# Building the adjacency: four of five tiles' slot one-hots scaled on ScalarE instead of three

## The chip, the cores and the metric

The kernel is one program on one core of a Trainium2 chip. The metric is the device time of one execution in microseconds (us). In the profile the engines are PE (TensorE matmuls), PEld (TensorE weight loads), DVE (VectorE), ACT (ScalarE), POOL (GpSimd) and SP (SyncE, which issues most DMAs).

## The reference

A two-stage graph network on 12500 nodes with 64 features and 412500 edges (`src`, `dst`, sorted by `dst`), cut to what matters:

```python
h = relu(layernorm(x))
x = x + hypergraph_conv2(h, (src, dst), W1, b1, W2, b2)   # segment sums over src and dst
h = relu(layernorm(x))
# e  = silu(silu([h[src], h[dst], edge_weight1] @ eW1 + eb1) @ eW2 + eb2)
# agg = segment_sum(e, src);  x = x + silu([h, agg] @ nW1 + nb1) @ nW2 + nb2
```

The change touches only the first stage of the kernel, called building here: it sorts the edges of each chunk of nodes into buckets, and counts them into blocks of the adjacency matrix, which the later stages read.

## The kernel before

Building takes the first 3.3 ms. It runs over 49 chunks (a turn of the loop each). A chunk holds `TC = 70` tiles of 128 edges, taken as `NGR = 14` groups of `GT = 5` tiles. Each engine has its own instruction stream, written by hand, and waits for the others on semaphores; nothing reorders the streams. I call the work that an engine's loop body does for one value of g a slot, so a turn has slots 0 to 13. For group g:

- **POOL** (`onehots`, L621) writes `OH`, for each edge a one-hot over 102 bucket keys.
- **PE** (`ranks`, L731 to L739) sums these into `R`, the running rank of each edge in its bucket. It does so one slot ahead.
- **ACT** copies the carry out of it (`count`, `cb`, L859) and widens `OH` to fp32 (`widen`, `OHf`, L865).
- **DVE** (`ranks`, L968 and L970) reduces `R` to the rank `rk` of each edge. Then `places` writes the slot one-hots of the group. For the first `AT` tiles it writes an unscaled bf16 one-hot `LB` (L981). For the others it writes `LH` itself, in one instruction a tile (L987): two one-hots, scaled by the edge's two payloads `pl`.
- **ACT** (`scaled`, L875) makes `LH` of the first `AT` tiles out of `LB`, with two activations a tile, one for each payload.
- **PE** (`buckets`, L753) multiplies `OHf` by `LH` into the sorted chunk `S`, with ten matmul rows a group, one slot later: in slot g + 1 it does `buckets` of group g.

The width of a one-hot, `WIDE[t]`, grows from 16 in the first tile to 128 in the last ones.

Between these, each of slots 2 to 13 has three or four units of the previous chunk (slots 0 and 1 have four each, the last of a chunk). For a unit, DVE writes the one-hots `OB`, `OA`, `OD` (L1038 to L1046, two units at a time), PE counts them into a PSUM bank (`counts`, L778, L779), ACT copies the bank into `RB` (`keep`, L911), and PE uses `RB` of a unit three back in `sums` (L794). At the end of a chunk DVE (`filled`, L999) and ACT (`record`, L882) empty `S`.

The order inside a slot matters below. PE in slot g: `ranks(g + 1)`, units 1 and 2, `buckets(g - 1)`, the other one or two units. ACT in slot g: `count(g + 1)`, `widen(g)`, `keep` of all units of the slot, then `scaled(g)`. DVE in slot g: two units, `ranks(g)`, one unit, `places(g)`, the rest. `LB`, `LH`, `OHf` and `cb` have two buffers each.

```python
for k in range(AT):                       # scaled, ACT, L871
    for c in range(2):
        ins = e.activation(LH[g % 2][:, k, c, 0:w], LB[g % 2][:, k, 0:w], ACT.Copy, scale=pl[:, c, t:t + 1])
ins.then_inc(a_lh, 1)
e.wait_ge(v_lh, i * NGR + (g + 1))        # buckets, PE, L745
e.wait_ge(a_of, i * NGR + (g + 1))
e.wait_ge(a_lh, i * NGR + (g + 1))
```

Of the kernel before, what the change touches and what calls it, by code (L numbers as in the profile page):

```python
# [20 lines left out]
TC = 70  # L21
CAP = TC * P
GT = 5
AT = 3
TWO = 2.0 ** -9
NGR = TC // GT
KEYS = 102
# [38 lines left out]
def gnn_kernel(nc, x, src, dst, ew, W1, b1, W2, b2, eW1, eb1, eW2, eb2, nW1, nb1, nW2, nb2, out):  # L66
# [14 lines left out]
    with root:  # L81
# [34 lines left out]
        def past(e, s, v):  # L116

            if not isinstance(v, int) or v > 0:
                e.wait_ge(s, v)

        def sbt(ctx, name, shape, dt):
            return ctx.enter_context(nc.sbuf_tensor(name, shape, dt))
# [353 lines left out]
        with tz:  # L476
            p1 = ExitStack()
            with p1:
# [7 lines left out]
                LH = [sbt(p1, f"LH{n}", [P, GT, 2, P], fp32) for n in range(2)]  # L486
                LB = [sbt(p1, f"LB{n}", [P, AT, P], bf16) for n in range(2)]
                OHf = [sbt(p1, f"OHf{n}", [P, GT, KEYS], fp32) for n in range(2)]
# [82 lines left out]
                with nc.Block() as block:  # L571
# [283 lines left out]
                    def _(e):  # L855
# [11 lines left out]
                        def scaled(i, g, pl):  # L867

                            e.wait_ge(v_lb, i * NGR + (g + 1))
                            past(e, p_s, i * NGR + (g - 1))  # L870
                            for k in range(AT):  # L871
                                t = g * GT + k
# [80 lines left out]
                    def _(e):  # L953
# [19 lines left out]
                        def places(i, g, pl):  # L973
# [4 lines left out]
                            past(e, a_lh, i * NGR + (g - 1))  # L978
                            for k in range(AT):
                                t = g * GT + k  # L980
                                ins = e.tensor_scalar(LB[g % 2][:, k, 0:WIDE[t]], iot1[:, 0:WIDE[t]], float(OWN - 1), rk[:, t:t + 1], ALU.add, ALU.is_equal)  # L981
                            ins.then_inc(v_lb, 1)
                            for k in range(AT, GT):
                                t = g * GT + k
# [1540 lines left out]
```

## Time and profile before

| | us |
|---|---|
| median of 3 runs | 9332.65 |
| lowest and highest | 9325.49, 9347.12 |
| the profiled execution, its own time | 9347.07 |
| its span | 9345.3 |

The span is the time from the first to the last instruction of the profiled execution. It lies 1.8 us inside that execution's own time, and that execution lies 14.4 us over the median. "Busy" counts the time in which an engine has an instruction at work; the ends of matmuls are modelled, their starts are recorded. Rows of the trace of before stand further down, in numbered groups.

### The profile page before, as it was taken

Reading aid. Unit: us, or ns where it says so; the run is one execution under the profiler, and the core shown is the slowest. Engines: PE = TensorE matmul, PEld = TensorE weight load, DVE = VectorE, ACT = ScalarE, POOL = GpSimd, SP = SyncE. Lnnn points to the kernel's source line nnn. Section 1 sums busy time; section 2 is a strip of 40 time slices with the busy share of each in tenths; the row PEclk is TensorE's granted clock in tenths of the full one; section 3 lists DMA queues with packets and bytes.
Section 4 is the critical chain, followed back from the end, with each engine's and each line's share of the span. In section 5 each row is a group of like instructions: output and inputs, shape, how many; then the busy total and the mean of one; then the engine's idle time right before and its main releaser. Section 6 shows DMA issues by size and latency. Waiting matters only on the chain. (4 is left out here: it accounts for less than half of the span.)

```text
span 9345.3 us, 289343 instructions
## 1 busy us (share of the span) xinstructions
PE 8577.7 (92%) x95106; PEld 7679.0 (82%) x95890; DVE 7760.4 (83%) x21596; ACT 5344.2 (57%) x14224; POOL 2985.7 (32%) x4177
## 2 busy tenths in 40 slices
PE   3999999999999989998888999599999999999997
PEld 2777777777777769998888998489989899999895
DVE  8999999999999976775888886478888888888884
ACT  3777777777777750001777786245555555555552
POOL 5877777777777830000000000011111111111110
PEclk9999999999999999997999998599999999999998
DMA  2666666666666677664999997533333333333332
GB/s 74 149 150 149 152 148 152 148 151 148 151 148 151 149 172 193 190 190 114 228 222 211 240 241 168 129 98 92 97 93 92 97 91 97 93 94 97 89 97 72
DMA packets 1475613, 1312.43 MB, mean 140 GB/s; under 512 B 829932, under 2 KB 1211094, under 8 KB 1473636
## 3 DMA queue, kind: packets, MB, share of 16 engines
q1 hardware_dynamic: 1444438, 1270.13, 56.3%
q0 software_dynamic: 28224, 26.62, 1.1%
q8 instruction: 739, 12.11, 0.5%
q14 instruction: 372, 3.05, 0.1%
q10 hardware_dynamic: 1840, 0.53, 0.0%
HBM read 777.40 MB, written 361.77 MB: 122 GB/s over the span
## 5 line engine op out<-in xcount | busy, mean ns | idle before, releaser
L621 POOL TENSOR_SCALAR OH<-iot,kd 128x102 bf16<-128x102 bf16 x3440 | 2334.1, 698 | 61.7 <-PE S L753 61.4
L2170 POOL DMA_INDIRECT Qx<-tab_q,tidx x294 | 407.5, 1386 | 5231.9 <-DVE skt L2204 2602.0
L1425 PE MATMUL wp<-AF,XS 128*128 128x256 f32 x9604 | 1214.6, 285 | 157.5 <-issue 121.7
L1425 PEld LDWEIGHTS wp<-AF,XS 128*128 128x128 f32 x9604 | 1165.9, 191 | 189.0 <-issue 188.8
L911 ACT ACTIVATE RB<-PS 128x256 int16<-128x256 f32 x2401 | 898.6, 381 | 639.9 <-PE PS L779 591.6
L1451 ACT ACTIVATE AF<-RG 128x1536 fp32r<-128x1536 uint8 x686 | 1022.6, 1491 | 340.9 <-PE wp L1425 208.0
L794 PE MATMUL HP<-T3a,RB 128*128 128x193 bf16 x9604 | 1187.3, 246 | 27.3 <-ACT RB L911 27.3
L753 PE MATMUL S<-LH,OHf 128*102 128x256 f32 (+14 forms) x6860 | 1160.5, 316 | 50.3 <-ACT LH L875 29.6
L2191 ACT ACTIVATE Z<-Zb 128x512 f32<-128x512 f32 x882 | 556.2, 631 | 991.6 <-DVE Zb L2249 987.6
L875 ACT ACTIVATE LH<-LB,pl 128x128 f32<-128x128 bf16 (+14 forms) x4116 | 1113.1, 356 | 0.0
L753 PEld LDWEIGHTS S<-LH,OHf 128*102 128x102 f32 x6860 | 921.7, 169 | 195.9 <-issue 96.1
L2249 DVE TENSOR_TENSOR Zb<-p,eb2s 128x512 f32<-128x512 f32 x882 | 609.9, 692 | 535.5 <-PE p L2143 502.1
L2143 PE MATMUL p<-eW2s,Y 128*128 128x128 f32 x7056 | 928.3, 274 | 48.9
L794 PEld LDWEIGHTS HP<-T3a,RB 128*128 128x128 fp8e4 x9604 | 851.7, 97 | 128.7 <-issue 39.8
L1505 DVE CAST AF<-RG 128x2048 fp32r<-128x2048 uint8 x686 | 813.3, 1222 | 155.7 <-DMA RG<-adjT 64.6
L2143 PEld LDWEIGHTS p<-eW2s,Y 128*128 128x128 f32 x7056 | 922.9, 191 | 24.1
L1046 DVE TENSOR_TENSOR OD<-iot,SBd 128x512 bf16<-128x512 bf16 x2401 | 937.4, 428 | 0.0
L2125 PEld LDWEIGHTS pT<-OdT,ACC 128*128 128x128 bf16 x21756 | 792.6, 97 | 162.1 <-issue 162.1
L2184 ACT ACTIVATE Y<-pT,eb1s 128x512 f32<-128x512 f32 x882 | 606.0, 687 | 494.8 <-PE pT L2125 462.8
L2125 PE MATMUL pT<-OdT,ACC 128*128 128x84 bf16 (+10 forms) x21756 | 853.0, 196 | 0.0
L1290 PE MATMUL hp<-ACC,RG 128*128 128x193 bf16 x9604 | 822.3, 247 | 4.0 <-DMA RG<-adjT 4.0
L1290 PEld LDWEIGHTS hp<-ACC,RG 128*128 128x128 fp8e4 x9604 | 815.0, 98 | 8.1 <-issue 4.5
(329 smaller groups left out, 16065.5 us busy)
## 6 DMA issues: line engine op xcount, KB each, us to landing
RG<-adjT SPq DMA_DIRECT2D x1372, 224.0 KB, 7.0
adj<-RB SPq DMA_DIRECT2D x343, 448.0 KB, 2.8
adjT<-RT SPq DMA_DIRECT2D x686, 224.0 KB, 3.7
RG<-adj SPq DMA_DIRECT2D x686, 224.0 KB, 4.6
sdb<-bk SPq DMA_DIRECT2D x196, 768.0 KB
sdb<-bk SPq DMA_DIRECT2D x98, 384.0 KB
sdb<-bk SPq DMA_DIRECT2D x98, 261.0 KB
WR<-wk SPq DMA_DIRECT2D x882, 9.0 KB
```

The costliest lines, as they stand in the source:

```text
L621: ins = e.tensor_scalar(OH[:, g * GT + k, :], iot1[:, 0:KEYS], kd[:, g * GT + k:g * GT + k + 1], None, ALU.is_equal)
L753: ins = e.matmul(slots_to(w), lhsT=OHf[g % 2][:, k, :], rhs=LH[g % 2][:, k, :, 0:w], start=False, stop=True, skip_group_check=True)
L794: ins = e.matmul(HP[:, h * W3:(h + 1) * W3], lhsT=pair[:, x_, h * P:(h + 1) * P], rhs=T3a[:, 2 * (u - 1) + x_, :], start=False, stop=True, ...
L875: ins = e.activation(LH[g % 2][:, k, c, 0:w], LB[g % 2][:, k, 0:w], ACT.Copy, scale=pl[:, c, t:t + 1])
L911: e.activation(RB[n % NSLOT][:, k, :].bitcast(i16), bank(u)[:, 0:256], ACT.Copy, accum_out=gs[:, u:u + 1]).then_inc(a_u, 1)
L1046: ins = e.tensor_tensor(OD[k % PAIRS][:, y, :, :], iot2[:, :, :], SBd[:, b + 2 * y:b + 2 * y + 2].unsqueeze(1).to_broadcast([P, 256, 2]), ...
L1290: ins = e.matmul(ps[b][:, h * W:(h + 1) * W], lhsT=piece(n, k_, h), rhs=tin3[:, n * 2 * PIECE + k_, 0:W], start=False, stop=True, skip_gro ...
L1425: ins = e.matmul(ps[b][:, 0:256], lhsT=XS[:, n * PB + m, :, :].rearrange("p c f -> p (c f)"), rhs=AF[:, (b + n) % 3, m, :], start=n == 0 a ...
L1451: e.activation(floats((b + n) % 3, VB, PB), counts(n, VB, PB), ACT.Copy).then_inc(h_ca, 1)
L1505: e.tensor_copy(floats((b + n) % 3, 0, VB), counts(n, 0, VB)).then_inc(h_cd, 1)
L2125: ins = e.matmul(o[:, a:b], lhsT=v[:, n, c, :], rhs=D_[:, h, a:b], start=False, stop=True, skip_group_check=True)
L2143: ins = e.matmul(p2[g % 2][:, t * P:(t + 1) * P], lhsT=Y[g % 2][:, t * P:(t + 1) * P], rhs=nW["eW2s"][:, :], start=True, stop=True)
```

## The change

`AT` goes from 3 to 4. `LB` grows by one tile, to `[P, AT, P]`.

```diff
@@ -21,7 +21,7 @@
 TC = 70
 CAP = TC * P
 GT = 5
-AT = 3
+AT = 4
 TWO = 2.0 ** -9
 NGR = TC // GT
 KEYS = 102
```

In each group the fourth tile's scaled pair, which one DVE instruction wrote (with `iofo`, an index row offset by 255), is now one bf16 one-hot from DVE and two activations on ACT. PE, POOL and SP keep every instruction in its place.

ACT, slots 12 and 13 of a turn in the loop (`RB` is `keep` of a unit, `LH<-LB,pl` is `scaled`), the second of them with four units:

```order
 L911 ACTIVATE RB,rows_of<-PS 128x256 x3
-L875 ACTIVATE LH<-LB,pl 128x128 x6
-L859 ACTIVATE cb<-R 128x102
-L865 ACTIVATE OHf<-OH 128x510
-L911 ACTIVATE RB,rows_of<-PS 128x256 x4
-L875 ACTIVATE LH<-LB,pl 128x128 x6
+L875 ACTIVATE LH<-LB,pl 128x128 x8
+L859 ACTIVATE cb<-R 128x102
+L865 ACTIVATE OHf<-OH 128x510
+L911 ACTIVATE RB,rows_of<-PS 128x256 x4
+L875 ACTIVATE LH<-LB,pl 128x128 x8
```

Each run of six activations is now a run of eight, and the signal that it is done comes with the eighth; the copy of the carry (`cb`) for the next group stands behind it.

DVE, slot 12 of the same loop (`LB` is the unscaled one-hot, `LH` the scaled pair, `OB` begins the next two units):

```order
-L981 TENSOR_SCALAR LB<-iot,rk 128x128 x3
-L987 SCALAR_TENSOR_TENSOR LH<-iofo,rk,pl 128x256
+L981 TENSOR_SCALAR LB<-iot,rk 128x128 x4
 L987 SCALAR_TENSOR_TENSOR LH<-iot,rk,pl 128x256
 L1038 TENSOR_SCALAR OB<-iot,SBk 128x128 x2
```

One instruction has taken the place of another; the signal for `LB` comes one instruction later, that for `LH` behind as many instructions as before.

## Rows read from the trace of the kernel before

**Rows 1.** The page: busy us, share of the span and instructions of each engine.

```profile
PE 8577.7 (92%) x95106; PEld 7679.0 (82%) x95890; DVE 7760.4 (83%) x21596; ACT 5344.2 (57%) x14224; POOL 2985.7 (32%) x4177
```

**Rows 2.** Busy time by stretch: bounds, length, engines, granted PE clock, DMA share, GB/s.

```profile
2000.00:2500.00 500.00, 474.96 (x4070) 393.03 (x4068) 480.30 (x2055) 389.60 (x1627) 380.21 (x566) 1.00 0.68 151
```

**Rows 3.** Timeline of PE, slots 12 and 13: start, length, instruction, idle before it.

```profile
1989.67 2.38 PE L753 MATMUL S<-LH,OHf 128*102 128x256 f32 x10 [0.36 <-ACT LH L875]
...
2051.56 2.32 PE L753 MATMUL S<-LH,OHf 128*102 128x240 f32 x10
...
2055.74 0.50 PE L794 MATMUL HP<-T3a,RB 128*128 128x193 bf16 x4
2056.60 2.38 PE L753 MATMUL S<-LH,OHf 128*102 128x256 f32 x10 [0.36 <-ACT LH L875]
```

**Rows 4.** Timeline of ACT in the same slots.

```profile
2049.59 1.82 ACT L875 ACTIVATE LH<-LB,pl 128x120 f32<-128x120 bf16 x6
...
2054.24 0.38 ACT L911 ACTIVATE RB<-PS 128x256 int16<-128x256 f32 x1 [1.44 <-PE PS L779]
...
2054.61 1.85 ACT L875 ACTIVATE LH<-LB,pl 128x128 f32<-128x128 bf16 x6
2056.36 0.23 ACT L859 ACTIVATE cb<-R 128x102 bf16<-128x102 f32 x1
```

**Rows 5.** Waits in building, 1000 to 3000 us (30 turns): total us, times, longest.

```profile
ACT RB L911 <- PE PS L779: 361.8, 390, 1.5
...
PEld S L753 <- issue: 56.7, 184, 0.6
...
PE PS L778 <- DVE OD L1046: 49.3, 60, 1.1
...
DVE rk L968 <- ACT cb L859: 32.1, 30, 1.1
...
PE S L753 <- ACT LH L875: 17.5, 60, 0.4
```

**Rows 6.** Groups of building by line (0 to 3300 us): count, busy us, mean ns.

```profile
L875 ACT ACTIVATE LH<-LB,pl 128x16 f32<-128x16 bf16 (+3 forms) x3990 | 1078.0, 356 | 0.0
...
L981 DVE TENSOR_SCALAR LB<-iot,rk 128x128 bf16<-128x128 bf16 (+14 forms) x1998 | 408.0, 267 | 25.1 <-DVE rk L970 17.5 <-PE S L753 3.9
...
L987 DVE SCALAR_TENSOR_TENSOR LH<-iofo,rk,pl 128x256 f32<-128x256 f32 (+11 forms) x666 | 257.8, 387 | 0.0
```

**Rows 7.** Timeline of DVE in slot 12: `places`, and the pair behind it.

```profile
2051.01 0.58 DVE L981 TENSOR_SCALAR LB<-iot,rk 128x128 bf16<-128x128 bf16 x3
2051.50 0.47 DVE L987 SCALAR_TENSOR_TENSOR LH<-iofo,rk,pl 128x256 f32<-128x256 f32 x1
2051.90 0.48 DVE L987 SCALAR_TENSOR_TENSOR LH<-iot,rk,pl 128x256 f32<-128x256 bf16 x1
```

**Rows 8.** Timeline of ACT: `scaled` of groups 2, 7 and 0, and what follows.

```profile
2007.81 1.42 ACT L875 ACTIVATE LH<-LB,pl 128x40 f32<-128x40 bf16 x6
2009.13 0.24 ACT L859 ACTIVATE cb<-R 128x102 bf16<-128x102 f32 x1
...
2029.38 1.65 ACT L875 ACTIVATE LH<-LB,pl 128x88 f32<-128x88 bf16 x6
...
2066.49 1.32 ACT L875 ACTIVATE LH<-LB,pl 128x16 f32<-128x16 bf16 x6
2067.69 0.27 ACT L859 ACTIVATE cb<-R 128x102 bf16<-128x102 f32 x1
```

**Rows 9.** Timeline of PE: where it waits for DVE, and `buckets` of groups 2 and 7.

```profile
2009.38 1.11 PE L753 MATMUL S<-LH,OHf 128*102 128x80 f32 x10 [0.23 <-ACT LH L875]
...
2019.81 0.29 PE L778 MATMUL PS<-OD,OA 128*128 128x256 bf16 x1 [0.93 <-DVE OD L1046]
...
2030.90 0.29 PE L778 MATMUL PS<-OD,OA 128*128 128x256 bf16 x1 [0.79 <-DVE OD L1046]
...
2032.03 1.71 PE L753 MATMUL S<-LH,OHf 128*102 128x176 f32 x10
```

## The prediction

> **What bounds the kernel now.** I read the busy shares first. Over the whole span PE is busiest, then DVE [rows 1], but the change lies in building alone, so the shares of that stretch count: of 500 us there, DVE is busy 480 and PE 475, while ACT is busy 390, or 78% [rows 2]. Read so far, DVE looks like the bound and ACT like the engine with room. A share does not say which wait ends last, so I went to the order of time.
>
> The turns repeat: `buckets` of group 12 starts at 1989.67 and again at 2056.60, 66.93 us apart [rows 3]. What releases it can be read from two timelines. ACT's six scaling activations of group 11 end at 2049.59 + 1.82 = 2051.41, and `buckets(11)` starts at 2051.56. Those of group 12 end at 2054.61 + 1.85 = 2056.46, and `buckets(12)` starts at 2056.60. Both times PE starts 0.14 to 0.15 us behind ACT's last activation [rows 3, 4]. It could have started sooner: four `sums` matmuls that began at 2055.74 take about 0.34 us from start to start, so PE was free at about 2056.1, and the profile gives the 0.36 us in between to `LH` of ACT [rows 3]. And ACT did not dawdle: it waited 1.44 us for PE's counts of the slot's last unit, copied them, and began to scale at once [rows 4].
>
> So in the late slots PE and ACT form a closed loop: `buckets` of one group, counts of the slot's last units, ACT's `keep`, ACT's `scaled`, `buckets` of the next group. DVE is not in it: its one-hots of group 12 stood from 2052.4 on, over 2 us before ACT read them [rows 7, 4]. The summed waits support this and also warn: PE's wait for `LH` is only 17.5 us in 30 turns, but another 56.7 us in 184 pieces, six a turn, stands at the same line under "issue" [rows 5], a name for idle time with no visible releaser. I take those for the same wait. ACT idles 361.8 us in 30 turns, all of it waiting for PE's counts [rows 5]. That is ACT's 22% of room, and it lies ahead of `keep`. The added work lies behind `keep`, so it cannot go there.
>
> DVE does set the time at two places of a turn: PE waits 0.93 us for `OD` at 2019.81 and 0.79 us at 2030.90 [rows 9], 49.3 / 30 = 1.64 us a turn on average [rows 5].
>
> **The change part by part.** *ACT, two activations more a group.* From the start of `scaled` to the start of the next instruction six activations take 1.32 us in slot 2 (2007.81 to 2009.13) and 1.75 us in slot 12 (2054.61 to 2056.36) [rows 8, 4]. The twelve distances of slots 2 to 13 grow with the width between these and sum to 18.85 us. Two more of eight cost a third of that: 6.28 us in twelve slots, of which slots 8 to 13 have 3.39. The group row gives the same size: 1078.0 / 3990 = 0.27 us each [rows 6], times 24 is 6.5.
>
> *DVE, one instruction exchanged a group.* `LB` costs 408.0 / 1998 = 0.20 us, the pair 0.387 us [rows 6]: 0.18 us saved a group, 2.6 us a turn. Start to start in slot 12 it is 0.49 / 3 = 0.16 against 0.40 [rows 7], so 0.24; with narrow one-hots less. `LB`'s signal comes 0.16 us later, hidden by the 2 us that it lies ready. SP, POOL and PE's work is unchanged; POOL has 120 of 500 us idle [rows 2].
>
> *What is late next, through one turn.* D is how much later PE is than before.
>
> 1. Slot 0: `scaled(0)` grows by 1.20 / 3 = 0.40 us (2066.49 to 2067.69), and the `cb` behind it is what DVE's next `ranks` waits for, 32.1 us in 30 turns [rows 5, 8]. Nothing covers it: both branches start 0.40 late. `scaled(1)` is followed by waits of ACT for PE, so I cost it at nothing; uncovered it would be another 0.4.
> 2. Slots 2 to 4: (1.32 + 1.38 + 1.43) / 3 = 1.38. `buckets(2)` has no slack (2007.81 + 1.42 + 0.15 = 2009.38, its start [rows 8, 9]); the next two have 0.15 together. D = 0.40 + 1.38 - 0.15 = 1.63.
> 3. The wait of 0.93 for `OD` absorbs that much: D = 0.70. DVE itself is no later than 0.40 less its savings there, three times 0.1 to 0.2, so it does not set the time.
> 4. Slots 5 and 6: (1.47 + 1.51) / 3 = 0.99, D = 1.69. The second wait for `OD`, 0.79, would take it to 0.90. But `scaled(7)`, which began at 2029.38 and took 1.65 [rows 8], now begins 1.69 later and takes 0.52 more: it ends at 2033.24, and `buckets(7)` starts 0.14 later, at 2033.38 instead of 2032.03 [rows 9]. D = 1.35.
> 5. Slots 8 to 13: all of them start 0.14 to 0.15 us behind ACT, as in rows 3 and 4, so their 3.39 goes in whole. D = 4.74.
>
> Over 30 turns the two waits average 1.64 us, not this turn's 1.72 [rows 5, 9], so other turns lose 0.1 more. I take 4.8 us a turn, 48 turns with both units and groups (the first has no units): 230 us. None of DVE's 2.6 us is in the sum, since DVE's stream is ahead wherever PE would use it. The end of DVE's turn waits for `buckets(13)` anyway, in `filled`.
>
> The profiled execution would then take 9347.07 + 230 = 9577 us; it lies 14.4 over the median of the runs, so the forecast is 9563.
>
> The clock: granted at 1.00 (2.4 GHz) in building, with PE 95% busy [rows 2]. With 5 us more idle in 67 PE would be at about 89%; I cost that at nothing.
>
> **The rivals.**
>
> *A: VectorE is the bound, and the change is a gain.* For it: the 480 of 500 us [rows 2], and PE's waits for `OD`. Then a turn shrinks by DVE's 2.6 us, 48 turns by 123: about 9210. From start to start the saving is nearer 2 us, giving 9237. Against it: the 0.14 us distances in slots 8 to 13, and DVE's own waits for ACT and PE at the turn's end. It decides if PE's matmuls of `buckets` could start before ACT is done, for which I see no row. The Trainium skill, Trace Analysis, "Identifying the Most-Contended Engine" and "Optimizing Scalar/DVE Operations", speaks for this rival: the engine with the highest occupancy is the one to relieve, and if DVE is saturated, work may go to Scalar. By that rule ACT's room would take the activations; the waits of rows 5 show where that room lies.
>
> *B: losses in the late slots only, and DVE's saving paid in full.* 3.39 - 2.6 = 0.8 us a turn, 38 us: 9371. It needs the early slots to be set by DVE throughout. Against it: `buckets(2)` waits for ACT too [rows 9].
>
> *C: the two cancel.* If the slots 2 to 7 gain what 8 to 13 lose: 9333. The same row speaks against it.
>
> *D: nothing absorbs.* 14 groups at 2 x 0.27 = 7.56 us a turn, 363 in all: 9696. The waits for `OD` would have to remain, which needs DVE to be later too.
>
> **How the numbers follow.** The loop of PE and ACT (forecast, 9563): 0.84. A 0.05, C 0.03, B 0.04, D 0.04. A measurement of this kernel tells some 0.2%, 19 us, from no change: faster 0.05, same 0.03, slower 0.92. The range: the low end takes 4.8 less DVE's 2.6, so 2.2 us a turn, or 106 us, 9438, which I raise a little to 9455, since it needs DVE's saving in full; the high end goes most of the way to D, 6.5 us a turn, or 312: 9645.
>
> **What would show it right or wrong.** After the change: turns of 71.5 to 72 us in place of 66.93; `scaled` of group 12 at about 2.4 us; `buckets` of late groups still 0.14 us behind it, now with 0.8 to 0.9 us idle ahead; PE's waits for `OD` gone or small; DVE busy near 88% of building, with longer waits for `cb` and `S`; ACT near 83%. A turn under 66.9 us, or late `buckets` that start before ACT's eighth activation, would prove me wrong; so would a `keep` that comes sooner than the counts allow.

## The result and the profile after

| | us |
|---|---|
| before, median of 4 runs | 9339.89 (9325.49 to 9351.01) |
| after, median of 4 runs | 9571.86 (9542.36 to 9616.22) |
| ratio after to before | 1.0252, 95% interval 1.0224 to 1.0279 |
| the profiled execution after: its time, its span | 9542.36, 9540.6 |

The change made the kernel 232 us slower. The forecast was 9563.

The page of after, the line that answers to [rows 1], and the stretch of building that answers to [rows 2] (busy us of PE, PEld, DVE, ACT, POOL, then granted clock, DMA share, GB/s):

```profile
PE 8563.1 (90%) x95106; PEld 7670.4 (80%) x95890; DVE 7672.2 (80%) x21596; ACT 5682.6 (60%) x15596; POOL 2910.0 (31%) x4177
```

```profile
2000.00:2500.00 500.00, 446.96 (x3775) 369.09 (x3773) 435.88 (x1913) 410.02 (x1704) 353.50 (x539) 1.00 0.63 140
```

DVE went from 480 to 436 us busy of 500, PE from 475 to 447. ACT, which got the work, went from 390 to only 410, since its added 28 activations a turn are spread over a longer turn. These are shares of equal stretches, and a turn is longer now (71.65 us for 66.93, below). For each turn DVE's busy time fell from 64.3 to 62.5 us, PE's stayed (63.6 and 64.0), and ACT's rose from 52.2 to 58.8. So of the 44 us that DVE lost in 500, most is the longer turn. No engine is saturated, and the kernel is slower. The granted clock is 1.00 still, so TensorE did not pay for its new idle time here.

The timeline of PE after (start, length, instruction, idle before it and its releaser), `buckets` of groups 12, 2 and 7, and 12 again, to set beside [rows 3, 9]:

```profile
1905.81 2.38 PE L753 MATMUL S<-LH,OHf 128*102 128x256 f32 x10 [0.94 <-ACT LH L875]
```

```profile
1926.93 1.11 PE L753 MATMUL S<-LH,OHf 128*102 128x80 f32 x10 [0.68 <-ACT LH L875]
...
1949.96 1.76 PE L753 MATMUL S<-LH,OHf 128*102 128x176 f32 x10 [0.47 <-DVE LH L987]
...
1977.46 2.38 PE L753 MATMUL S<-LH,OHf 128*102 128x256 f32 x10 [0.94 <-ACT LH L875]
```

A turn takes 71.65 us (1905.81 to 1977.46) in place of 66.93. The wait ahead of `buckets(12)` grew from 0.36 to 0.94, so by 0.58: two activations. The row of group 7 names DVE's `LH`, but ACT's timeline shows which came last: its run of eight for group 7 in the next turn ends at 2019.30 + 2.18 = 2021.48, and `buckets(7)` starts at 2021.62.

The timeline of ACT after, groups 7 and 12, to set beside [rows 4, 8]:

```profile
2019.30 2.18 ACT L875 ACTIVATE LH<-LB,pl 128x88 f32<-128x88 bf16 x8
...
2046.12 0.38 ACT L911 ACTIVATE RB<-PS 128x256 int16<-128x256 f32 x1 [1.44 <-PE PS L779]
...
2046.49 2.43 ACT L875 ACTIVATE LH<-LB,pl 128x128 f32<-128x128 bf16 x8
2048.83 0.23 ACT L859 ACTIVATE cb<-R 128x102 bf16<-128x102 f32 x1
```

```profile
2021.62 1.76 PE L753 MATMUL S<-LH,OHf 128*102 128x176 f32 x10 [0.47 <-ACT LH L875]
...
2049.07 2.38 PE L753 MATMUL S<-LH,OHf 128*102 128x256 f32 x10 [0.94 <-ACT LH L875]
```

ACT's idle time ahead of the last `keep` is 1.44 us, as before. The two activations come after it: `scaled(12)` takes 2.34 us from start to start, where it took 1.75, and PE starts 0.15 us behind its end (2046.49 + 2.43 = 2048.92, 2049.07).

Summed waits after, 1000 to 3000 us (28 turns), which answer to [rows 5]:

```profile
ACT RB L911 <- PE PS L779: 284.6, 335, 1.5
PEld S L753 <- issue: 226.7, 288, 1.1
...
PE S L753 <- ACT LH L875: 176.3, 314, 0.9
DVE rk L968 <- ACT cb L859: 74.6, 101, 1.5
DVE LB L981 <- PE S L753: 70.7, 56, 1.4
```

PE's wait for ACT's `LH` rose from 17.5 to 176.3 us, and the piece at the same line under "issue" from 56.7 to 226.7. The second is the same wait as TensorE's weight loads (PEld) show it, so the two must not be added. First a late `buckets` of before, `buckets(11)`, which in PE's own row of [rows 3] has no idle time, then `buckets(12)` of after, with 0.94 us in PE's row:

```profile
2051.53 1.93 PEld L753 LDWEIGHTS S<-LH,OHf 128*102 128x102 f32 x10 [0.31 <-issue]
```

```profile
1905.78 1.98 PEld L753 LDWEIGHTS S<-LH,OHf 128*102 128x102 f32 x10 [1.14 <-issue]
```

PE's waits for `OD` are no longer listed. DVE waits for a buffer that PE's `buckets` must free, 2.5 us a turn: the time that it saved it spends, in part, in front of this buffer.

All of the loss is in building. The last `buckets` (the line's own view: last start) began at 3405.4 us before and here at 3637.4, 232.0 later:

```profile
L753 PE MATMUL S<-LH,OHf x6860: 192/313/635, 156.2 to 3637.4; 128*102 128x32 f32 x49, 128*102 128x112 f32 x49, 128*102 128x176 f32 x49, 128*102 128x240 f32 x49
```

The rest of this one profiled execution is 37 us shorter than in the one of before (9540.6 - 3637.4 = 5903.2 against 9345.3 - 3405.4 = 5939.9), in code that the change does not touch. Part of it may be the clock: two stretches of a later stage, first of before, then of after, both 2295 us behind the last `buckets`, show a mean granted clock of 0.69 and 0.75, between its two levels of 1.2 GHz (0.5) and 2.4 GHz (1.0). The longest stretch at 1.2 GHz in that stage lasts 314 us before and 249 us after.

```profile
5700.00:6200.00 500.00, 372.52 (x3139) 331.74 (x3167) 269.04 (x413) 185.68 (x266) 20.77 (x15) 0.69 0.48 118
```

```profile
5932.00:6432.00 500.00, 366.76 (x3645) 330.69 (x3685) 290.50 (x474) 194.69 (x292) 24.58 (x18) 0.75 0.49 121
```

So the profiled executions differ by 195 us, and the medians by 232. Below I give, beside each ratio, the shift of the last `buckets`, which such later differences do not touch. It comes from one profiled execution of each kernel; how far it varies from one execution to the next was not measured.

### The profile page after: what moved, and what is told of

It reads as the page before. It is cut to its first block and busy times, and to the rows that moved or that the text cites. A ratio compares the mean times of both kernels' runs of the same rounds, so it can differ in the third digit from the quotient of the medians.

```text
span 9540.6 us, 290715 instructions
## 1 busy us (share of the span) xinstructions
PE 8563.1 (90%) x95106; PEld 7670.4 (80%) x95890; DVE 7672.2 (80%) x21596; ACT 5682.6 (60%) x15596; POOL 2910.0 (31%) x4177
## 5 line engine op out<-in xcount | busy, mean ns | idle before, releaser
L621 POOL TENSOR_SCALAR OH<-iot,kd 128x102 bf16<-128x102 bf16 x3440 | 2281.1, 681 | 321.9 <-PE S L753 321.9
L875 ACT ACTIVATE LH<-LB,pl 128x128 f32<-128x128 bf16 (+14 forms) x5488 | 1465.0, 356 | 0.0
L2125 PEld LDWEIGHTS pT<-OdT,ACC 128*128 128x128 bf16 x21756 | 792.8, 97 | 162.1 <-issue 162.1
```

What stands on the lines that cost most here:

```text
L621: ins = e.tensor_scalar(OH[:, g * GT + k, :], iot1[:, 0:KEYS], kd[:, g * GT + k:g * GT + k + 1], None, ALU.is_equal)
L2125: ins = e.matmul(o[:, a:b], lhsT=v[:, n, c, :], rhs=D_[:, h, a:b], start=False, stop=True, skip_group_check=True)
```

## The experiments

The theory: PE and ACT form a closed loop (`buckets`, counts of the slot's last units, `keep`, `scaled`, `buckets`). What ACT does behind its last `keep` of a slot lengthens the loop, and what it does ahead of it is free. The main rivals: time goes by the busiest engine, or by ACT's total work.

### The same ACT work at two places

Two activations a group, as wide as the fourth tile, are added to the kernel before. They write a buffer that nobody reads. **Behind** the keeps:

```diff
 def scaled(i, g, pl):
+    for c in range(2):
+        e.activation(idle[:, g % 2, c, 0:WIDE[g * GT + 3]], iot1[:, 0:WIDE[g * GT + 3]], ACT.Copy, scale=onef[:, 0:1])
     e.wait_ge(v_lb, i * NGR + (g + 1))
```

> The kernel before, with two more activations a group on ACT that write a buffer nobody reads, as wide as the fourth tile, placed behind the slot's keeps and just ahead of scaled. DVE is as before. Theory (PE and ACT form a closed loop from buckets over counts, keep and scaled to the next buckets, and what lies behind keep lengthens it): a turn grows by nearly as much as with the change, 4.7 us, 9565 us in all (ratio 1.024). Rival (ACT has 22% of room and the time goes by VectorE): ratio 1.000 to 1.003. Rival (the order of the fourth tile's data, not ACT's work, costs the time): ratio near 1.000.

Measured: 9581.36 us, ratio 1.0263 (1.0239 to 1.0288); the last `buckets` 231.3 us later. **Ahead** of them, the same two instructions right behind `widen`:

```diff
     e.activation(OHf[g % 2][:, :, :], OH[:, g * GT:(g + 1) * GT, :], ACT.Copy).then_inc(a_of, 1)
+    for c in range(2):
+        e.activation(idle[:, g % 2, c, 0:WIDE[g * GT + 3]], iot1[:, 0:WIDE[g * GT + 3]], ACT.Copy, scale=onef[:, 0:1])
```

> The same two activations a group, but placed right behind widen, ahead of the slot's keeps. ACT's total work is that of act_behind. Theory: ACT idles 0.2 to 1.5 us for PE's counts later in each slot, so most of them are hidden; slots 1, 3 and 4 of a turn, with little idle, lose about 0.4 us together: 10 to 40 us in all, ratio 1.001 to 1.004. Rival (what counts is ACT's total work, wherever it lies): the same as act_behind, 1.024.

Measured: 9344.02 us, ratio 1.0002 (0.9985 to 1.0019); the last `buckets` at 3402.8 us, 2.6 us sooner than before. The two timelines of ACT, first behind, then ahead, in a late slot:

```profile
2047.12 0.38 ACT L914 ACTIVATE RB<-PS 128x256 int16<-128x256 f32 x1 [1.44 <-PE PS L780]
...
2047.49 0.68 ACT L871 ACTIVATE idle<-iot,onef 128x128 f32<-128x128 bf16 x2
2048.07 1.85 ACT L878 ACTIVATE LH<-LB,pl 128x128 f32<-128x128 bf16 x6
```

```profile
2054.27 0.68 ACT L868 ACTIVATE idle<-iot,onef 128x128 f32<-128x128 bf16 x2
...
2056.53 0.38 ACT L914 ACTIVATE RB<-PS 128x256 int16<-128x256 f32 x1 [0.85 <-PE PS L780]
...
2056.90 1.85 ACT L878 ACTIVATE LH<-LB,pl 128x128 f32<-128x128 bf16 x6
```

Ahead, the pair is taken out of ACT's idle time before the last `keep` (0.85 us is left of some 1.4). Behind, the idle time stays at 1.44 and the pair goes into the loop. The same work costs 231 us or nothing. This settles the rival of ACT's total work. It also shows that the whole loss comes without any change on DVE and without the fourth tile's data taking another path. I had charged the version ahead 10 to 40 us, for slots with little idle time; it cost nothing that can be measured. PE's waits for `OD` were smaller with it, by 15 us in 30 turns (49.3 before, [rows 5]), which is 0.5 us a turn, or 24 us in 48:

```profile
PE PS L779 <- DVE OD L1049: 34.2, 60, 0.8
```

That they took in what I had charged fits this, and was not tried by itself.

### VectorE loaded again

The changed kernel, with one more scaled pair a group on DVE, to a buffer that nobody reads:

```diff
     ins.then_inc(v_lb, 1)
+    t = g * GT + 3
+    w = WIDE[t]
+    e.scalar_tensor_tensor(idle[:, g % 2, :, 0:w], iofo[:, 0:w].unsqueeze(1).to_broadcast([P, 2, w]),
+                           rk[:, t:t + 1], pl[:, :, t:t + 1].to_broadcast([P, 2, w]), ALU.is_equal, ALU.mult)
     for k in range(AT, GT):
```

> The changed kernel, with one more scaled pair a group written by DVE to a buffer nobody reads, as wide as the fourth tile (0.39 us each by the group row, 5.4 us a turn), between LB's signal and LH. Theory (DVE's stream is ahead wherever PE would use it; DVE is busy 62 of 71.6 us): within 0.5% of the changed kernel, ratio to before 1.025 to 1.030. Rival (DVE sets part of the time, and its saving is in the result): 5.4 us x 48 = 259 us more, ratio about 1.05.

Measured: 9596.29 us, ratio 1.0286 (1.0253 to 1.0320); the last `buckets` at 3657.3, 20 us later than in the changed kernel. DVE got some 5.4 us a turn of work (5.5 by the new row's 153.1 us in 28 turns) and the turn grew by 20 / 48 = 0.4 us. So DVE is close to being out of the picture after the change, though not wholly.

### The change, half by half

`AT` is 4 in groups 8 to 13 only (`late4`), and in groups 0 to 7 only (`early4`). The loops of `scaled` and of `places` go by `FOUR(g)`:

```diff
-AT = 3
+AT = 4
+def FOUR(g):
+    return 4 if g >= 8 else 3      # early4: g < 8
...
-                            for k in range(AT):
+                            for k in range(FOUR(g)):
```

> Four tiles on ACT only in groups 8 to 13, three in groups 0 to 7. By the prediction's step 5 these six slots have no slack at all: 3.39 us a turn, 163 us, ratio 1.017; the last buckets of building start 163 us later than before (there 3405.4 us). Rival (VectorE's saving counts): six groups save it 1.3 us a turn, so about 100 us or less.

Measured: 9522.29 us, ratio 1.0187 (1.0167 to 1.0206); the last `buckets` at 3567.5 us, 162.1 later (163 expected).

> The other half: four tiles on ACT only in groups 0 to 7. By steps 1 to 4 part of their 3.3 us a turn vanishes in PE's two waits for OD and in slot 7's slack: 1.35 to 1.6 us a turn, 65 to 77 us, ratio 1.007 to 1.008. If the steps are right in kind this and late4 add up to the change's 232 us. Rival (nothing is absorbed): 3.3 us x 48 = 158 us.

Measured: 9410.95 us, ratio 1.0079 (1.0059 to 1.0099); the last `buckets` at 3471.8 us, 66.4 later (65 to 77 expected). The line's view of the two, `late4` first:

```profile
L759 PE MATMUL S<-LH,OHf x6860: 192/313/634, 156.0 to 3567.5; 128*102 128x32 f32 x49, 128*102 128x112 f32 x49, 128*102 128x176 f32 x49, 128*102 128x240 f32 x49
```

```profile
L759 PE MATMUL S<-LH,OHf x6860: 192/313/433, 156.3 to 3471.8; 128*102 128x32 f32 x49, 128*102 128x112 f32 x49, 128*102 128x176 f32 x49, 128*102 128x240 f32 x49
```

162.1 + 66.4 = 228.5, against 232.0 for both at once. The late slots lose all that is put into them, 3.38 us a turn. The early ones lose 1.38 of about 3.3. The six late groups save DVE their share of its work as well, and the sum of 3.39 has nothing for that.

### The other direction

> Two tiles a group on ACT instead of three: the step in the other direction from the kernel before. ACT's part of the loop is 6.3 us a turn shorter, and DVE has 2 to 2.6 us more to do, with 2.4 us of idle time in a turn before. Theory: DVE now sets the time, and only its waits for cb and S shrink: -0.5 to +1.5 us a turn, ratio 0.997 to 1.008, with PE's waits for OD several times larger. Rival (the loop of PE and ACT alone sets the time of the kernel before): 4 to 6 us a turn less, ratio 0.97 to 0.98.

With `AT = 2` (9405.02 us, ratio 1.0062, 1.0042 to 1.0082; the last `buckets` at 3477.1, 71.7 later) the kernel is slower than before as well. One stretch of building, and the waits of 1000 to 3000 us:

```profile
2000.00:2500.00 500.00, 461.48 (x3954) 381.68 (x3952) 488.63 (x2000) 329.98 (x1375) 379.34 (x566) 1.00 0.66 146
```

```profile
PEld PS L778 <- DVE OD L1046: 156.7, 217, 1.5
PE PS L778 <- DVE OD L1046: 110.2, 172, 1.2
```

Now DVE is the bound, busy 489 of 500 us, and PE waits for `OD` more than twice as long as before (110.2 against 49.3, [rows 5]). In the order in which the streams were written, three tiles were the balance between two limits: one tile more costs 4.7 us a turn at the loop, one tile less 1.5 at DVE.

### ACT's room used where it lies

If position is all, the four-tile version can be made to pay. `scaled` is cut in two, and its first `EARLY` tiles are put ahead of the slot's third `keep`:

```diff
+                                early = EARLY if rank and len(us) > 2 else 0
                                 for n, u in enumerate(us):
+                                    if n == 2 and early:
+                                        scaled(i, g, pl[b], 0, early)
...
                                 if rank:
-                                    scaled(i, g, pl[b])
+                                    scaled(i, g, pl[b], early, AT)
```

The signal `a_lh` comes with the last tile. Two tiles early, of four:

> The changed kernel, with scaled cut in two: the four activations of the first two tiles go ahead of the slot's third keep, where ACT idles for PE's counts, the other four stay behind the last keep. Theory: the loop of PE and ACT then holds four activations a slot, two fewer than before the change, and DVE has its 2 to 2.6 us a turn less; PE's own work becomes the bound: a turn of 64 to 65 us, 9200 to 9270 us in all, faster than the kernel before by 0.7 to 1.5%. Rival (ACT's total work counts): as the changed kernel, 1.025.

Measured: 9221.49 us, ratio 0.9868 (0.9843 to 0.9894); the last `buckets` at 3282.2, 123.2 us sooner than before. A turn is then 66.93 - 123.2 / 48 = 64.4 us, inside the 64 to 65 expected. ACT in one late slot, that of group 11 (two units, the early activations, two more units, the late activations), and PE's `buckets(11)`:

```profile
2044.60 1.25 ACT L877 ACTIVATE LH<-LB,pl 128x120 f32<-128x120 bf16 x4
2046.27 0.38 ACT L914 ACTIVATE RB<-PS 128x256 int16<-128x256 f32 x1 [0.42 <-PE PS L780]
...
2047.21 1.26 ACT L877 ACTIVATE LH<-LB,pl 128x128 f32<-128x128 bf16 x4
```

```profile
2048.89 2.28 PE L754 MATMUL S<-LH,OHf 128*102 128x240 f32 x10
```

The first four activations fill the idle time ahead of the third `keep`, 0.42 us of it is left, and the last four end at 2047.21 + 1.26 = 2048.47, before PE gets to `buckets` at 2048.89. That row has no idle time in front. The loop no longer binds in this slot, and DVE's saving counts. That PE's own work is now the bound, as I had expected, is not shown: from 2000 to 2500 us PE is busy 486 us and DVE 487, and PE still waits for `OD`, 34.1 us from 1000 to 3000 us.

With one and with three of the four tiles early:

> The changed kernel with one of the four scaled tiles ahead of the third keep, so that six activations stay behind the last keep, as in the kernel before the change. DVE has its 2 to 2.6 us a turn less than before. Theory (with six behind, the loop is what it was, and DVE's saving can only shorten the two waits for OD and what follows them): 0 to 1.7 us a turn less than before, ratio 0.992 to 1.000. Rival (DVE sets the time of the kernel before throughout): 2 to 2.6 us a turn, ratio 0.987.

Measured: 9323.26 us, ratio 0.9982 (0.9968 to 0.9997); the last `buckets` at 3388.0, 17.4 us sooner. Six activations behind the last `keep`, as before the change, give nearly the old time, although DVE has its 2 us a turn less to do. That is what DVE's saving alone is worth while the loop stands: 0.4 us a turn. Set against `act_ahead`, which has as many activations ahead of the last `keep` and DVE's full work, it is 3402.8 - 3388.0 = 14.8 us, or 0.3 a turn.

> The changed kernel with the first three of the four scaled tiles ahead of the slot's third keep, one behind. Theory: with at4_early2 the loop of PE and ACT hardly binds any more (PE waits 7.9 us for ACT's LH in all of building); six activations take 1.3 to 1.75 us, more than ACT's idle time there, and delay the keeps: within 0.3% of at4_early2 (0.987), on either side. Rival (the loop still binds): another 0.5 us a slot less, ratio 0.980 or lower.

Measured: 9200.64 us, ratio 0.9868 (0.9843 to 0.9893); the last `buckets` at 3265.0, 140.4 sooner. By the ratio it is level with two early. By the medians it is 21 us ahead (9200.64 against 9221.49), by the last `buckets` 17, but the four runs of each overlap. Both are inside the 0.3% expected.

Three tiles, two of them early, so that DVE keeps the fourth pair:

> The kernel before (three tiles on ACT), with the first two tiles' four activations ahead of the slot's third keep. Theory: the loop of PE and ACT holds only two activations a slot, so DVE with its 64.2 us of work a turn sets the time: a turn of 65 to 66 us, 45 to 90 us less than before, ratio 0.990 to 0.995; less gain than at4_early2 (0.987), since here VectorE keeps the fourth tile's pair. Rival (DVE's share of the work plays no part): at least as fast as at4_early2.

Measured: 9291.89 us, ratio 0.9947 (0.9928 to 0.9966); the last `buckets` at 3346.6, 58.8 sooner. Here the move of the fourth tile from DVE to ACT, which costs 232 us in the old order, is worth 123.2 - 58.8 = 64 us in the new one.

All five tiles on ACT, three early, with no `LH` from DVE at all:

> All five tiles on ACT, the first three ahead of the third keep, two behind; DVE writes no scaled pair at all. Theory: ACT has then 78% x 66.9 + 28 x 0.51 = 66 us of work a turn and becomes the bound: a turn of at least 66 us, ratio 0.995 to 1.010, slower than at4_early2. Rival (DVE still sets the time): another 2 to 2.6 us a turn off at4_early2, ratio 0.975.

Measured: 9246.96 us, ratio 0.9902 (0.9877 to 0.9927); the last `buckets` at 3313.8, 91.6 sooner. The direction against `at4_early2` was right and the size was not. One stretch of building, and the activations' row of 1000 to 3000 us:

```profile
2000.00:2500.00 500.00, 487.22 (x4181) 407.68 (x4180) 465.35 (x2109) 493.07 (x2101) 373.55 (x587) 1.00 0.71 154
```

```profile
L879 ACT ACTIVATE LH<-LB,pl 128x128 f32<-128x128 bf16 (+14 forms) x4319 | 1233.1, 408 | 0.0
```

ACT is the bound, as I expected, busy 493 of 500 us. But a turn is 66.93 - 91.6 / 48 = 65.0 us, of which ACT is busy 64.1, and my sum had been 66.5. I had added up busy times. In the timeline of before, the instruction that ends each `keep` (ACTIVATION_READ_ACCUMULATOR) lasts 0.19 to 0.20 us, but when work follows, the next one starts 0.09 us after its start. Ahead of idle time its whole length counts as busy, and in an ACT without pauses half of it lies under the next instruction. A turn of before has 16 such pieces of idle time, so I estimate 1.6 us of tails. That is the larger part of the 2.4 us that the sum was too high; the rest is open. The work of an engine that is to be filled is smaller than its busy time.

## Why the prediction was right, by its steps

The forecast, slower by 230 us in building (9563), met 232.0 by the last `buckets` and 9571.86 by the median. The reading that ACT's late activations release `buckets`, and that ACT's room lies ahead of `keep`, is shown by the pair of `act_behind` and `act_ahead`. One reading of the rows was too wide: of ACT's idle time in those 30 turns, 449 us, only the 361.8 us lie ahead of `keep`; 53.1 us more are its wait for DVE's `vi` ahead of `record`. So the room ahead of `keep` was 18% and not 22%. No sum used it. Taking the 56.7 us under "issue" for the same wait as PE's was right (the PEld rows above).

Step by step, from `buckets(12)` of one turn, which puts the 0.58 us of group 13 (step 5) at the front. To `buckets(2)` it was 2009.38 - 1989.67 = 19.71 us and is 21.12 (1926.93 - 1905.81): 1.41 later. Steps 5 (one group), 1 and 2 give 0.58 + 0.40 + 0.44 = 1.42. At `buckets(4)` the delay is 2.26, and at `buckets(5)`, behind the first wait for `OD`, it is down to 1.71; the steps give 2.21 and 1.77. To `buckets(7)`, 42.36 became 44.15: 1.79 later, where steps 1 to 4 give 0.58 + 1.35 = 1.93. To the next `buckets(12)`, 66.93 became 71.65: 4.72, where the ledger had 4.74 for this turn and 4.8 for the mean. What the early slots lose in all (steps 1 to 4) is measured by `early4`: 1.38 us a turn, with 1.35 in the ledger. Step 5, that late slots lose all, is measured by `late4`: 3.38 of 3.39.

DVE's saving at nothing: right for the changed kernel, since a load of twice the saving costs it only 0.4 us a turn. `act_behind` says the same: it has the change's ACT work and none of DVE's saving, and its last `buckets` is 231.3 us late against 232.0. With the loop as it was before, the saving is not quite nothing: 0.3 to 0.4 us a turn by `at4_early1`.

What was foreseen in the profile came: turns of 71.5 to 72 us (71.65), `scaled(12)` at about 2.4 (2.43), DVE near 88% (87%), ACT near 83% (82%), PE's waits for `OD` gone. The idle time ahead of late `buckets` was given as 0.8 to 0.9 us. It goes from 0.59 us in group 8 to 0.94 in group 12; before, only group 12 of these had idle time listed (0.36), so a growth of some 0.57 us does not end at one value. The sum did not depend on it.

Rival A, VectorE as the bound, fell: relieving DVE by 1.8 us a turn (64.3 to 62.5) went with a longer turn, and `dve_load` put work back at almost no cost. That rival had the rule of the Trainium skill, Perfetto Trace Analysis, "Identifying the Most-Contended Engine", on its side: DVE had the highest occupancy in building. The runs do not bear it out for this order of work. They do once the loop is cut: from `at3_early2` to `at4_early2` the same move of work off DVE is a gain. The same page of the Trainium skill, in "Optimization Strategy", asks for the semaphore that the gaps of the engine in question wait on, and put to PE's gaps ahead of `buckets` that is the reading that held here. Rival B's low sum, 38 us, and C's, zero, fell with `early4`, which loses 66 us and does not gain. D, with nothing absorbed, fell with it too.

## What to carry to other kernels

Before work is moved to an engine with room, look at where in its stream the room lies: idle time ahead of an instruction that waits is free for work put ahead of it, and work put behind it pays in full if the next engine waits for the result. The sign to look for is a start that stands at the same short distance behind another engine's end, slot after slot (here 0.14 to 0.15 us), even where the sum of the listed waits is small. A balance found by trying one number (here two, three or four tiles) holds for one order of the stream alone: with `scaled` cut in two, four tiles are 1.3% faster than the kernel before, and in the old order 2.5% slower.

## What was not expected of the hardware

ACT's instructions grow longer, by the profile, where ACT hardly pauses. The activations of one width, 128, from 1000 to 3000 us, first of before, then of `at5_early3`:

```profile
L875 ACT ACTIVATE LH<-LB,pl 128x128 f32<-128x128 bf16 x420 | 131.4, 389 | 0.0
```

```profile
L879 ACT ACTIVATE LH<-LB,pl 128x128 f32<-128x128 bf16 x806 | 265.0, 452 | 0.0
```

The mean length of one went from 389 to 452 ns, but the busy time for each only from 131.4 / 420 = 0.313 to 265.0 / 806 = 0.329 us. Within `at5_early3` the length climbs in a stretch without a pause and falls back behind a short one, while the distance to the next start stays:

```profile
2003.65 0.32 ACT L916 ACTIVATION_READ_ACCUMULATOR RB<-PS 128x1 f32 x1
2003.75 0.48 ACT L916 ACTIVATE RB<-PS 128x256 int16<-128x256 f32 x1
...
2016.40 0.20 ACT L916 ACTIVATION_READ_ACCUMULATOR RB<-PS 128x1 f32 x1
2016.50 1.30 ACT L879 ACTIVATE LH<-LB,pl 128x16 f32<-128x16 bf16 x6
```

The same instruction lasts 0.32 and 0.20 us, and the next starts 0.10 us behind its start both times. The row's mean length is then the wrong price for one more instruction; the distance from start to start is the right one. Why the length grows was not tried.
